# A recurrent layer beside a mixture of experts: the skip term x·D joins the sums over states, chunk by chunk

## What is computed

```python
xn = _layernorm(x, axis=-1)
s = _L0_attn_ref(xn, ...)          # state-space branch
g = _silu(_L0_ffn_ref(xn, ...))    # mixture of 8 experts, top 2
x = x + s * g

# inside _ssm_forward, with x = xn:
x_conv = silu(causal conv of 4 taps over time)
a = jnp.exp(delta[..., None] * A[None, None])
b = delta[..., None] * B_in[:, :, None, :] * x_conv[..., None]
h = a_t * h + b_t                       # scan over time, 16 states per channel
y = jnp.einsum('btdn,btn->btd', h_all, C_in) + x * D_param

# inside the experts: 1024 rows each, gelu(x @ fc1 + b1) @ fc2 + b2, times the gate
```

## Time and profile before

| what | value |
|---|---|
| median of three runs | 2011.69 us |
| the profiled execution | 2014.59 us |
| its span | 2012.7 us |
| PE busy | 1847.6 us (92%) |
| DVE busy | 1853.9 us (92%) |
| POOL busy | 1303.5 us (65%) |
| ACT busy | 1222.6 us (61%) |
| mean of the DMA | 119 GB/s |

### The profile page before, as it was taken

How to read it: one execution, slowest core, us unless ns; L and a number is a source line. 1 busy time by engine, 2 the same in 40 slices (tenths; PEclk the granted TensorE clock), 3 DMA queues, 4 the chain that set the end, 5 groups by cost and what they waited for, 6 DMA issues and landing times. The chain is left out here.

```text
span 2012.7 us, 29247 instructions
## 1 busy us (share of the span) xinstructions
PE 1847.6 (92%) x8968; PEld 1449.4 (72%) x8968; DVE 1853.9 (92%) x2004; ACT 1222.6 (61%) x1772; POOL 1303.5 (65%) x621
## 2 busy tenths in 40 slices
PE   6998189999999999999999999999999999999940
PEld 3332078888888878887888788888888888888830
DVE  7998579899998999899989998999899989999899
ACT  3577585556755665566556655666565755675543
POOL 1388466578667776677567866786678667866530
PEclk9999699999999999999999999999999999999975
DMA  9168643346212531244124511351145113621396
GB/s 315 68 97 114 172 173 116 115 162 153 74 64 103 138 86 61 73 146 109 63 73 142 120 68 64 124 121 63 63 150 127 63 63 111 177 74 63 108 355 242
DMA packets 83894, 240.06 MB, mean 119 GB/s; under 512 B 11713, under 2 KB 12609, under 8 KB 71505
## 3 DMA queue, kind: packets, MB, share of 16 engines
q1 hardware_dynamic: 67120, 205.07, 31.1%
q0 software_dynamic: 16416, 33.70, 9.2%
q10 hardware_dynamic: 256, 0.26, 0.1%
HBM read 170.45 MB, written 68.55 MB: 119 GB/s over the span
## 5 line engine op out<-in xcount | busy, mean ns | idle before, releaser
L1188 DVE TENSOR_TENSOR_SCAN a_sb<-a_sb,state,ub_sb 128x512 f32<-128x512 f32 x512 | 894.2, 1785 | 9.9 <-issue 6.0
L1097 POOL TENSOR_TENSOR ub_sb<-u_sb,brow_sb 128x1024 f32<-128x1024 f32 x256 | 629.5, 2459 | 401.7 <-DVE a_sb L1188 398.9
L829 PE MATMUL pm<-xTh,w1l 128*128 128x512 f32 x1024 | 423.0, 413 | 6.8 <-POOL w1l L1082 5.7
L829 PE MATMUL pm<-w2h,hl 128*128 128x512 f32 x1024 | 422.8, 413 | 0.2 <-DVE hl L1168 0.2
L831 PE MATMUL pm<-w2h,hh 128*128 128x512 f32 x1024 | 401.8, 392 | 0.0
L831 PE MATMUL pm<-xTh,w1h 128*128 128x512 f32 x1024 | 401.6, 392 | 0.0
L830 PE MATMUL pm<-w2l,hh 128*128 128x512 f32 x1024 | 398.6, 389 | 0.0
L830 PE MATMUL pm<-xTl,w1h 128*128 128x512 f32 x1024 | 398.1, 389 | 0.0
L1159 DVE SCALAR_TENSOR_TENSOR s_acc_keep<-pt,ct_keep,s_acc_keep 128x512 f32<-128x512 f32 x480 | 352.0, 734 | 19.7 <-PE pt L861 19.0
L976 ACT ACTIVATE a_sb<-delta_sb,neg_a_keep 128x512 f32<-128x512 f32 x512 | 330.2, 713 | 6.7
L861 PE MATMUL pt<-ident_keep,a_sb 128*128 128x128 f32 x2048 | 306.3, 272 | 5.7 <-DVE a_sb L1188 5.7
(11 more groups left out here) (163 smaller groups left out, 1950.8 us busy)
## 6 DMA issues: line engine op xcount, KB each, us to landing
raw_keep<-in_w SPq DMA_DIRECT2D x64, 1024.0 KB, 4.8
brow_sb<-b_chunks SPq DMA_DIRECT2D x128, 256.0 KB
moe_rows<-zeros SPq DMA_DIRECT2D x8, 1280.0 KB, 6.4
xn_rows<-xn_sb SPq DMA_DIRECT2D x8, 1024.0 KB, 9.1
delta_chunks<-ln_sb SPq DMA_DIRECT2D x8, 1024.0 KB
u_chunks<-xn_sb SPq DMA_DIRECT2D x16, 512.0 KB
delta_sb<-delta_chunks SPq DMA_DIRECT2D x8, 1024.0 KB, 8.1
u_sb<-u_chunks SPq DMA_DIRECT2D x16, 512.0 KB, 3.9
```

The source lines that it names most:

```text
L829: pe.matmul(out, sl, mh, start=start, stop=False)
L1097: pool.tensor_tensor(ub[:, h], u[:, 2 * h:2 * h + 2, :], brow[:, m % 2:m % 2 + 1, :].to_broadcast([P, 2, CH]), ALU.mult).then_inc(s_["bmul ...
L1188: op = dve.tensor_tensor_scan(abuf[:, m, 2 * h + k, :], abuf[:, m, 2 * h + k, :], ub[:, h, k, :], state[:, ds(col, 1)], ALU.mult, ALU.add)
```

## The change

The skip term is no longer computed in the tail. In the two middle quarters (q = 1, 2) of each of the first seven chunks, the normalised rows of the next chunk are read from `xn_rows` into `b2`, one block of 128 rows at a time, multiplied with D by GpSimd after its products i = 4 and i = 7, and stored to a new tensor in memory, `skip_rows`. In the first quarter of the next chunk SP loads each block from there into `s_acc`, behind the store of the sums that were there. The sum over states then adds to it from its first state on. The rows of chunk 0 are loaded into `s_acc` straight from `xn_rows` and multiplied with D by VectorE, in four steps of its first quarter.

In the tail, `normalise`, `scale` and `add_skip` are gone, `gate` waits for the loads itself, the last four parts of the experts' output go where the normalised parts were, and SP issues all 16 loads of them ahead of all 16 stores. On SP and POOL the two middle quarters are now written out, with the same content apart from the new pieces.

```diff
@@ SP, new functions
+                def load_skip(tb):
+                    if begins(e):
+                        sp.wait_ge(s_["x_turned"], TPC + tb + 5)
+                    else:
+                        sp.wait_ge(s_[f"s_out{tb}"], 16 * e)
+                        sp.wait_ge(s_[f"ahead_out{tb}"], 16 * e)
+                    src = dr.xn if begins(e) else dr.skip
+                    sp.dma_start(s_acc[:, tb, :], src[ds(e * CH + tb * P, P)]).then_inc(s_[f"skip_in{tb}"], 16)
+                def before(q, k):
+                    return TPC * e + 2 * (q - 1) + k
+                def fetch_ahead(q, k):
+                    if k == 0:
+                        sp.wait_ge(s_["biased"], TILES * (e + 1) + 1)
+                    tb = 2 * (q - 1) + k
+                    if tb > 0:
+                        sp.wait_ge(s_[f"ahead_out{tb - 1}"], 16 * e + 16)
+                    elif not begins(e):
+                        sp.wait_ge(s_["ahead_out3"], 16 * e)
+                    apart(sp, s_["sp_at"])
+                    sp.dma_start(b2[:], dr.xn[ds((e + 1) * CH + (2 * (q - 1) + k) * P, P)]).then_inc(s_["ahead_in"], 16)
+                def store_ahead(q, k):
+                    sp.wait_ge(s_["ahead"], before(q, k) + 1)
+                    sp.dma_start(dr.skip[ds((e + 1) * CH + (2 * (q - 1) + k) * P, P)], b2[:]).then_inc(s_[f"ahead_out{2 * (q - 1) + k}"], 16)
@@ SP, a quarter
                     load_b(it, q, 0)
+                    ahead = 1 <= q < NQ - 1 and not ends(e)
+                    if ahead:
+                        fetch_ahead(q, 0)
...
                     weights(it, 1)
                     load_b(it, q, 1)
-                    if first and not begins(e):
-                        for tb in range(TPC):
-                            store_s(tb)
+                    if first:
+                        for pair in ((0, 1), (2, 3)):
+                            if not begins(e):
+                                for tb in pair:
+                                    store_s(tb)
+                            if pair[0] == 0:
+                                for tb in pair:
+                                    load_skip(tb)
                     for m in range(2, NPQ):
                         load_b(it, q, m)
+                        if ahead and m == 2:
+                            store_ahead(q, 0)
+                        if ahead and m == 3:
+                            fetch_ahead(q, 1)
+                            store_ahead(q, 1)
+                        if first and m == 2:
+                            for tb in (2, 3):
+                                load_skip(tb)
@@ SP, the tail
-            for p in range(NP - 4):
+            for p in range(NP):
                 load_y(p)
-            for p in range(2):
-                store(p)
-            for p in range(NP - 2, NP):
-                load_y(p)
...
+            for p in range(NP):
                 store(p)
@@ GpSimd, behind each product ub i
+                        if 1 <= q < NQ - 1 and not ends(e) and i in (4, 7):
+                            k = 0 if i == 4 else 1
+                            if i == 4:
+                                pool.wait_ge(s_["d_row"], 16)
+                            pool.wait_ge(s_["ahead_in"], 16 * (TPC * e + 2 * (q - 1) + k) + 16)
+                            apart(pool, s_["pool_at"])
+                            pool.tensor_tensor(b2[:], b2[:], d_row[:], ALU.mult).then_inc(s_["ahead"], 1)
@@ VectorE
                 if starts:
-                    dve.wait_ge(s_[f"s_out{tb}"], 16 * e + 16)
-                    dve.tensor_scalar(acc, h, c, None, ALU.mult).then_inc(s_["summed"], 1)
-                else:
-                    dve.scalar_tensor_tensor(out=acc, in0=h, scalar=c, in1=acc, op0=ALU.mult, op1=ALU.add).then_inc(s_["summed"], 1)
+                    if begins(e):
+                        dve.wait_ge(s_["skipped"], tb + 1)
+                    else:
+                        dve.wait_ge(s_[f"skip_in{tb}"], 16 * e + 16)
+                dve.scalar_tensor_tensor(out=acc, in0=h, scalar=c, in1=acc, op0=ALU.mult, op1=ALU.add).then_inc(s_["summed"], 1)
+            def skip(e, tb):
+                dve.wait_ge(s_[f"skip_in{tb}"], 16 * e + 16)
+                dve.tensor_tensor(s_acc[:, tb, :], s_acc[:, tb, :], d_row[:], ALU.mult).then_inc(s_["skipped"], 1)
```

More of the change, by code:

```diff
@@ L652, in main_loop @@
             b2_in staged add_staged added0 added1 cleared biased carried act_at dve_at pool_at sp_at
-            d_row zeroed shift xn skip whole silu gated sum out
+            d_row zeroed skip_in0 skip_in1 skip_in2 skip_in3 skipped ahead_in ahead ahead_out0 ahead_out1 ahead_out2 ahead_out3 silu gated sum out
             """ + " ".join(f"x_chunk{c} s_chunk{c} y_part{2 * c} y_part{2 * c + 1}" for c in range(NCH)))
@@ L659, in main_loop @@
         y_rows = ([abuf[:, m] for m in range(NPQ)] + [part[:, 0:TPC, :], part[:, TPC:, :]] +
[L660 to L665, removed]
+                  [late[:, 11], ub[:].rearrange("p h k d -> p (h k) d")])
         LAST = NQ * NCH
@@ L767, in quarter @@
                         load_x(0)
-                quarters(e, sp, quarter)
+                for q in range(NQ):
+                    quarter(e * NQ + q, q, q == 0, q == NQ - 1 and not ends(e))
             chunks(sp, chunk)
@@ L1016, in _ @@
             chunks(act, chunk)
[L1018 to L1026, removed]
             def silu(p):
@@ L1030, in silu @@
                 act.activation(half(y_rows, p), half(y_rows, p), ACT.Silu).then_inc(s_["silu"], 1)
[L1032 to L1036, removed]
             for p in range(NP):
@@ L1109, in quarter @@
                                 gather(e + 1, t)
-                quarters(e, pool, quarter)
+                for q in range(NQ):
+                    quarter(e * NQ + q, q, q == 0, q == NQ - 1 and not ends(e))
             chunks(pool, chunk)
@@ L1198, in quarter @@
                             sum_up(e, q, s, first, last)
+                        if first and begins(e) and LAG <= s + 1 < LAG + TPC:
+                            skip(e, s + 1 - LAG)
                         if s < 8:
@@ L1209, in _, with gate @@
                 sum_up(NCH, 0, s, True, False)
[L1211 to L1217 removed]
+            def gate(p):
                 if p < NP - 2:
                     dve.wait_ge(s_[f"s_chunk{p // 2}"], 16)
[L1220 to L1224 removed]
                 dve.wait_ge(s_["silu"], p + 1)
@@ L1230, in add_x @@
                 dve.tensor_tensor(half(x_rows, p), half(x_rows, p), half(s_rows, p), ALU.add).then_inc(s_["sum"], 1)
-            dve.wait_ge(s_["d_row"], 16)
             dve.wait_ge(s_["summed"], GROUPS * NCH + 4)
-            scale(0)
-            for p in range(NP):
-                if p + 1 < NP:
-                    scale(p + 1)
-                add_skip(p)
             gate(0)
```

26 lines of the change are left out of this document (5 added, 21 removed).

## The result

| what | before | after |
|---|---|---|
| median, us (4 runs each, same chip) | 2011.82 | 2097.07 |
| lowest and highest, us | 2011.02 to 2016.66 | 2096.45 to 2102.54 |
| ratio, 95% interval | | 1.0415 [1.0399, 1.0432] |
| span of the profiled execution, us | 2012.7 | 2094.6 |
| first and last matmul of the main loop, us | 254.4 and 1934.7 | 253.6 and 2034.8 |

The changed kernel is slower by 85 us. The forecast said slower by 38 us, with a range up to 2088 us: the sign was right, and the time lies 9 us above the range. The spans differ by 81.9 us: the start is 0.8 us shorter, the main loop 100.9 us longer (1680.3 to 1781.2 us), and the tail 18.2 us shorter (78.0 to 59.8 us). So the tail gave somewhat more than forecast, and the loop cost about twice as much.

A forecast was written before the change was run, and what follows sets the result against it. TensorE was taken to bound the main loop and DVE the tail. Stalls 53.2 + chunk 0 1.2 - tail 15.7 = +38.7 us, against the median of 2011.7 us: 2050 us, range 2028 to 2088 us.

The forecast's parts named there:

- What bounds the kernel: TensorE bounds the main loop, so each wait put on it is added whole; DVE bounds the tail.
- The chain on SP: Middle quarters: w1's load waits behind the second product's store; ub 7 to TensorE's start takes 19.0 us.
- The stall's length: TensorE stalls 4.0 us at q = 2 and 3.6 us at q = 3, in seven chunks: 53.2 us.
- third rival: Loop: DVE runs ahead, ub 7 comes earlier and stalls shrink; 1997 us with the stall gone entirely; chance 0.07.
- The sum without the clock: Whole kernel: 53.2 + 1.2 - 15.7 = +38.7 us, with nothing added for half clock after stalls.
- The first rival: Middle quarters: TensorE's clock falls to half in each stall, 33 us more, 2083 us; chance 0.25.
- The port: Middle quarters: GpSimd's D products hold up DVE, alone at most 9.4 us; added as 0 since TensorE stalls anyway.
- Chunk 0's multiplications: Chunk 0's first quarter: four DVE multiplications, about 0.6 us each, cost TensorE 0 to 2.3 us, taken as 1.2.
- First quarters: First quarters: blocks loaded into the sums behind the stores arrive in time and nothing waits: 0.
- The tail: Tail: 32 of DVE's 64 instructions go; 15.7 us gained, between 14.6 and 21.5 us.

The follow-up runs named there:

- The first two experiments: Changed kernel with the second product's store behind the next w1 and B loads: 2002.23 us, ratio 0.9932; changed kernel with that product behind ub 6: 2023.4 us, 1.0034.
- the second experiment: Changed kernel with the second product of a middle quarter behind ub 6 instead of ub 7, SP's order kept: 2023.4 us, ratio 1.0034.

## Why the prediction was half right

**What bounds the kernel: right.** In the loop TensorE's waits and the half clock behind them make up 99.8 of the 100.9 us, and in the tail what DVE was spared came back.

**The chain on SP: right.** The forecast counted 19.0 us from the start of ub 7 to TensorE's restart; it took 19.13 us (1249.69 to 1268.82), and 19.4 us in the next quarter. Its terms held: the product 1.29 us (taken 1.2), store to next issue 0.69 (0.65), issue to split 5.63 (5.4), split 1.92 (1.92). The first two experiments show that this chain is the cause of the stalls.

**The stall's length: right in kind, too small.** The forecast took 4.0 and 3.6 us, from a restart that was due 15.0 and 15.4 us after ub 7. Chunks 1 to 6 had 50.5 us of stalls, 8.4 us a chunk instead of 7.6. In the quarter shown TensorE was ready 14.3 us after ub 7 (1268.82 less the wait of 4.83, less 1249.69), where it had been 15.0 before, so ub 7 stood later against TensorE, not earlier: there DVE did not run ahead (third rival). In the next quarter it was 15.7 us against 15.4, which is as good as no change. Why ub 7 moved in the first of the two, no run tells. Chunk 0 was taken like the others, and had 14.7 us: the forecast did not look at what else chunk 0's queue holds, the zeros. Together this term was 65.2 us instead of 53.2.

**The sum without the clock: the step that failed.** The forecast priced each stall at its length and put the clock's fall into a rival of 0.25, because 4.0 and 3.6 us lay at the edge of 3.8 us, which it had read from one event at TensorE's end. One event is no edge: the clock fell with fourteen of fourteen stalls, the shortest of 3.70 us, and the fall came at anything from 1.8 to 5.3 us after TensorE had stopped. It cost 27.4 us by the rows, and the experiment that kept TensorE busy took 20.4 of such 25.2 us away. With the 12.0 us by which the stalls were too small this is what put the time outside the range: 27.4 + 12.0 = 39.4 us of the 43.2 between the loss forecast and the 81.9 us of the spans. The first rival was the right mechanism. Its own size was too high, 2.35 us a stall against 2.0, and its sum, 2083 us, missed by 14 us, of which chunk 0's longer stalls are 7.1 (14.7 less 7.6). That 2083 with the 12.0 us added comes to 2095 us, near the measured 2097, is in part luck, since its clock is 5.5 us too dear, its tail 2.5 us too long, and chunk 0's first quarter too cheap.

**The port: right.** It was added at 0, and the run with the products alone is 14.5 us under the kernel before, against the 14.8 us without them.

**Chunk 0's multiplications: too small.** They were taken at 0.6 us each, 1.2 us for TensorE. Two of the four took over 2 us, beside GpSimd; DVE in chunk 0 of the changed kernel:

```profile
276.62 2.22 DVE L1189 TENSOR_TENSOR s_acc_keep<-s_acc_keep,d_row 128x512 f32<-128x512 f32 x1
...
286.04 2.48 DVE L1189 TENSOR_TENSOR s_acc_keep<-s_acc_keep,d_row 128x512 f32<-128x512 f32 x1
...
289.70 0.68 DVE L1189 TENSOR_TENSOR s_acc_keep<-s_acc_keep,d_row 128x512 f32<-128x512 f32 x1
```

TensorE's wait for DVE grew by 3.0 us, and the clock's fall behind it cost 1.7 us more: 4.7 us, twice the upper bound of 2.3. The term should have been priced with the port, as the scans were the earlier trace rows, and with the clock.

**First quarters: right.** No wait of TensorE on a sum came with the loads into `s_acc`.

**The tail: right.** 18.2 us instead of 15.7, inside the bounds of 14.6 and 21.5. The first load of y landed about 9.6 us after its issue instead of 11.1 us, and the table for silu was loaded at 2008.47 us, long before, where the forecast had 1.28 us for it on the path.

Adding the terms as measured: 65.2 + 27.4 + 3.0 + 1.7 + 2.5 - 18.2 = 81.6 us, against 38.7 forecast and 81.9 in the spans. Open is the rest of 1.1 us in the loop, and the start that is 0.8 us shorter.

## What to carry to other kernels

Where a change puts a wait into a queue that issues in order, list what stands behind it there before asking what the new work costs: 28 products that cost nothing as work cost over 90 us through one store ahead of one load. Moving that store behind two loads took this cost away and left 12.8 of the 18.2 us that the tail gives; most of the difference is chunk 0's first quarter, which has its own new work and its own fall of the clock. Price a stall of TensorE with the time at half clock behind it, and count the stretches that differ from the rule (the first chunk) apart. One observed event gives no edge; where a term lies near one, the price with it belongs into the sum or into an even chance.

## What the hardware showed that I had not expected

- The clock falls with short stalls, and sometimes only after work is back. The stall at q = 3 in the windows' chunk is 3.75 us long; TensorE restarts at 1325.45 us, and the clock is still full for most of the next microsecond. The windows of the changed kernel:

```profile
1325.20:1326.20 1.00, 0.75 (x3) 0.67 (x4) 1.00 (x1) 1.00 (x2) 1.00 (x2) 1.00 0.00 0
1326.20:1327.20 1.00, 1.00 (x5) 0.82 (x5) 1.00 (x2) 0.98 (x3) 1.00 (x2) 0.88 0.94 131
1327.20:1330.00 2.80, 2.80 (x9) 2.11 (x9) 0.37 (x1) 1.35 (x3) 2.64 (x2) 0.50 0.94 392
1330.00:1332.00 2.00, 2.00 (x11) 1.71 (x10) 1.34 (x2) 1.11 (x2) 1.70 (x2) 0.91 0.46 137
```

  The half-speed level begins about 1.5 us after the restart, and it lasts as long as behind the stall of 4.83 us. The Trainium skill ("TensorE: Matmul & The Clock Gate", section "HAM oscillation — how this bites in real kernels") describes a kernel that waits for a DMA in every K-tile (a piece of its sum) and starts each of them cold, that is at half clock. This trace agrees in that half clock goes with each of its fourteen stalls, and differs in that three of them were followed by 1.3 to 1.5 us of work at full clock first. Which shorter waits spare the clock has no single edge in these runs. It stayed full behind all waits of 1.9 us and less in the second experiment. PE's wait for `hl` in chunk 0 is 2.8 to 2.9 us long in ten of the profiles: the clock fell with it in eight, the changed kernel's among them, and stayed full in two, those of the second experiment and of the one with the zeros ahead. So one event of either kind proves little.
- GpSimd's own instructions stretch beside DVE too: ub and the low piece of w1, 2.4 us alone, took 3.39 and 3.28 us in the second experiment, the first of them beside a pair of DVE's scans that took 4.56 us. The forecast had looked at DVE's side of the port only.
- Doing more work on TensorE made the kernel faster, by 23.2 us in the medians and 17.0 us in the main loops of the two profiled executions, since the clock stayed up.
